# Attention in another order within its step, and one chain of Newton turns for two sets of row scalars

## The chip, the core and the metric

The kernel runs on one core of a Trainium2 chip. The time is device time in microseconds from start to end of one launch. The core has a matrix engine (TensorE, PE in the profile), a vector engine (VectorE, DVE), a scalar engine (ScalarE, ACT), GpSimd (POOL), and SyncE (SP), which here only issues transfers. Each engine works through its own instructions in the order in which they were written, and waits at an instruction until the semaphores that it names have reached a value.

## What is computed

Eight sequences of 512 tokens with 128 channels go through three residual stages: a mixture of experts, linear attention, and the same mixture of experts again.

```
x = x + 0.5 * ffn(layernorm(x))
x = x + attention(layernorm(x))
x = x + 0.5 * ffn(layernorm(x))

attention: q, k, v = x @ W.T + b, 16 heads of 8;  q = elu(q) + 1;  k = elu(k) + 1
           kv = sum_t k v ;  den = q . sum_t k ;  out = (q kv / max(den, 1e-6)) @ Wo.T + bo
ffn:       logits = x @ wg; the 2 best of 8 experts per token, each with room for 1024 tokens,
           h = relu(x @ w1 + b1); y = h @ w2 + b2; out = sum of the two, weighted
```

The second layernorm and routing work on the sum that attention leaves, so each sequence must be through attention before its tokens can be ranked and sent to their experts.

## The kernel before, in words

The program has four blocks: the first routing, the first experts, attention (with the second routing woven in), and the second experts. The change is in the attention block, at 171 to 308 us of the profiled execution.

**The step.** Attention goes over the NG = 8 sequences ("groups"), each as GT = 4 tiles of 128 tokens, in steps s = 0 to 7 and a tail. One step handles several groups in different phases. For the newest group s: VectorE adds the two expert results that GpSimd gathered (L910, `add_rows`), takes statistics (L1511), and works out the row scalars of the layernorm by three turns of a Newton iteration on 128x4 tiles (`scale_steps`, L1520 to L1547: each instruction waits for the one before it). ScalarE applies them (`norm`, L1431), TensorE turns the rows (`turn`, L1321), ScalarE copies them out (`anT_out`, L1439), TensorE makes q (L1328) and k, v (`kv`, L1337), ScalarE computes the exponentials (L1447 to L1461), and VectorE completes q and k (`q_sum` L1562, `k_sum` L1556). For group s-1: the key sum (`keysum`, L1349), the masking (`kv_mask`, L1569) and the answers (`query`, L1357). For group s-2: the division on VectorE (L1574 to L1585), the turning back (`turn_out`, L1365), the output projection (`project`, L1373 and L1377), the residual addition (L1591) and the statistics for the second routing (L1597). For s-3 and s-4: `route.turn` (L490), its copy (L449), and the routing's logits (`row_logits`, L502).

**The second routing** works in parts of two groups. Part 0 has its row scalars (`row_scalar_steps`, L273 to L315) in step 4 and its ranking (`top2_steps`, L586 to L620) in step 5; part 1 in steps 6 and 7; parts 2 and 3 in the tail. After a ranking, TensorE counts (`counts`, L742 to L749), and VectorE places and marks the rows (`place_steps`, `mark_steps`, to L822).

**GpSimd's queue.** It gathers 8 tiles for each group (L1269), one after another; after the last of them it sends the rows of part 0, 16 transfers (L839), and then those of parts 1 and 2 as they are marked. The second experts' block reads its first rows when these 48 are in.

**Order.** It is written out by hand: in `tensor`, `scalar` and `vector` of `Attention`, in a loop over s. On VectorE `advance(scale, n)` issues n more steps of the Newton chain at that place, `finish` all that are left. `fill` is a TensorE matmul on a constant, whose result is not used (L1312). Transposes of attention (L1321) and of the second routing (L490) share one bank of the accumulator memory (bank 0).

## Time and profile before

| | us |
|---|---|
| median of 3 runs | 473.25 |
| lowest and highest | 467.95, 474.01 |
| the profiled execution's own time | 469.24 |
| its span, first to last instruction | 467.5 |
| PE busy | 360.9 (77%) |
| DVE busy | 351.7 (75%) |
| POOL busy | 278.6 (60%) |
| ACT busy | 236.8 (51%) |

No engine is busy throughout. The chain that ended last is 54% PE, 11% DVE, 7% DMA and 6% POOL over the whole span; the shares are an average over stages with different limits, and the steps of attention have to be read by themselves. "Granted clock" is the share of full speed at which TensorE ran: 1.00 is 2.4 GHz, 0.50 is 1.2 GHz, and the trace has no other level.

### The profile page before, as it was taken

How to read it: one execution, taken by the hardware profiler on the slowest of the kernel's cores; microseconds unless marked ns; L12 is line 12 of the kernel's file. 1: busy time of each engine (PE TensorE's matmuls, PEld its weight loads, DVE VectorE, ACT ScalarE, POOL GpSimd, SP SyncE). 2: the span in 40 equal slices, each digit the busy share in tenths (PEclk: the TensorE clock that was granted, in tenths of full speed). 3: DMA queues.
4: the chain of work that ended last, by engine and by line, in shares of the span. 5: the costliest groups of instructions: out<-in, count | busy, mean ns of one | idle time of the engine just before them, and what ended most of it. 6: DMA issues, size and time to landing. Idle time of an engine off the chain costs nothing.

```text
span 467.5 us, 6299 instructions
## 1 busy us (share of the span) xinstructions
PE 360.9 (77%) x1830; PEld 287.1 (61%) x1830; DVE 351.7 (75%) x1083; ACT 236.8 (51%) x431; POOL 278.6 (60%) x303
## 2 busy tenths in 40 slices
PE   7932879999999975889877978505799999999300
PEld 6912548888888733667665758405588888888200
DVE  6889178998888864688878885840489889889483
ACT  3688147667776604455354471420466776666100
POOL 9000577666664457777754636677767777776720
PEclk9999989999999989799889795756899999999855
DMA  8940314666666341121110101111622232311599
GB/s 229 356 159 1 96 46 133 208 201 194 222 225 219 117 131 51 52 57 51 53 45 25 53 25 52 52 57 58 202 69 77 82 93 90 92 46 41 163 326 296
DMA packets 47265, 55.50 MB, mean 119 GB/s; under 512 B 6694, under 2 KB 32832, under 8 KB 47232
## 3 DMA queue, kind: packets, MB, share of 16 engines
q1 hardware_dynamic: 34352, 35.40, 22.9%
q0 software_dynamic: 8512, 17.60, 12.9%
q10 hardware_dynamic: 4368, 2.10, 1.5%
q8 instruction: 15, 0.25, 0.2%
q14 instruction: 18, 0.15, 0.1%
HBM read 25.98 MB, written 29.10 MB: 118 GB/s over the span
## 4 chain that ended last, share of the span: by engine, by line
PE 54%; DVE 11%; DMA 7%; POOL 6%; ACT 6%; issue 4%; POOLq 0%; ACTq 0%; DVEq 0%; SPq 0%
PE psum L1056 6%; PE psum L1052 6%; PE psum L1069 6%; PE psum L1067 6%; PE psum L1068 6%; PE psum L1053 6%; PE psum L1078 3%; PE psum L1039 3%; POOL xg L1025 3%; PE psum L1357 2%; PE psum L1312 2%; DMA xs_dram<-xns,place 2%; PE psum L1337 2%; DMA xns<-yt_dram 2%; ACT an L1431 2%
## 5 line engine op out<-in xcount | busy, mean ns | idle before, releaser
L1121 ACT ACTIVATE hf<-psum,bcol 128x512 f32<-128x512 f32 x128 | 88.5, 691 | 64.8 <-PE psum L1056 61.6
L1025 POOL DMA_INDIRECT xg<-xn_dram,gidx x64 | 68.0, 1062 | 67.1 <-POOLq L1702 37.5
L1158 DVE TENSOR_TENSOR hl<-hf,hh 128x512 fp32r<-128x512 f32 x128 | 87.2, 691 | 5.1 <-ACT hh L1123 2.2
L1011 POOL DMA_INDIRECT yt_dram<-yg,target x64 | 74.2, 1159 | 27.7 <-issue 16.6
L839 POOL DMA_INDIRECT xs_dram<-xns,place x64 | 63.5, 992 | 40.0 <-DMA xs_dram<-xns,place 15.7
L1269 POOL DMA_INDIRECT yg<-y_dram,slot x64 | 61.2, 957 | 30.2 <-issue 19.3
L1052 PE MATMUL psum<-xh,wres 128*128 128x512 f32 x128 | 54.1, 422 | 3.4 <-ACT xh L1106 3.4
L1067 PE MATMUL psum<-hh,wres 128*128 128x512 f32 x128 | 53.0, 414 | 0.0
L1056 PE MATMUL psum<-xl,wres 128*128 128x512 f32 x128 | 51.4, 402 | 0.1
L1053 PE MATMUL psum<-xh,wres 128*128 128x512 f32 x128 | 50.9, 398 | 0.0
L1069 PE MATMUL psum<-hh,wres 128*128 128x512 f32 x128 | 50.5, 395 | 0.0
L1068 PE MATMUL psum<-hl,wres 128*128 128x512 f32 x128 | 50.2, 393 | 0.0
L1151 DVE CAST hh<-hf 128x512 fp32r<-128x512 f32 x96 | 44.3, 462 | 6.3 <-ACT hf L1121 5.8
L1147 DVE TENSOR_TENSOR xl<-psum,xh 128x512 fp32r<-128x512 f32 x32 | 21.9, 683 | 31.0 <-ACT xh L1106 31.0
L1106 ACT CAST xh<-psum 128x512 fp32r<-128x512 f32 x32 | 18.8, 587 | 30.7 <-PE psum L1039 28.8
L1312 PE MATMUL psum<-ones_bf 128*128 128x512 bf16 x94 | 27.9, 428 | 2.2 <-PEq L1796 2.2
L1052 PEld LDWEIGHTS psum<-xh,wres 128*128 128x128 f32 x128 | 24.5, 192 | 8.3 <-ACT xh L1106 4.4
L1056 PEld LDWEIGHTS psum<-xl,wres 128*128 128x128 f32 x128 | 24.5, 192 | 7.2 <-DVE xl L1147 1.8
L1069 PEld LDWEIGHTS psum<-hh,wres 128*128 128x128 f32 x128 | 24.2, 189 | 5.5
L1053 PEld LDWEIGHTS psum<-xh,wres 128*128 128x128 f32 x128 | 24.7, 193 | 4.2
L1068 PEld LDWEIGHTS psum<-hl,wres 128*128 128x128 f32 x128 | 24.3, 190 | 4.2
L1067 PEld LDWEIGHTS psum<-hh,wres 128*128 128x128 f32 x128 | 24.3, 190 | 3.7
(247 smaller groups left out, 726.3 us busy)
## 6 DMA issues: line engine op xcount, KB each, us to landing
yt_dram<-zeros SPq DMA_DIRECT2D x24, 256.0 KB, 3.5
xns<-yt_dram SPq DMA_DIRECT2D x24, 256.0 KB, 5.0
xs_dram<-zeros SPq DMA_DIRECT2D x16, 288.0 KB, 2.7
xg<-xs_dram SPq DMA_DIRECT2D x16, 288.0 KB, 2.8
wexp_raw<-in_L_ffn_w SPq DMA_DIRECT2D x16, 256.0 KB, 6.2
y_dram<-y_rows_out SPq DMA_DIRECT2D x16, 256.0 KB, 2.4
x_sb<-in_L_attn_x SPq DMA_DIRECT2D x8, 256.0 KB, 4.1
xn_dram<-xns SPq DMA_DIRECT2D x8, 256.0 KB, 5.9
```

The source lines that it names most:

```text
L839: gp.indirect_dma_start(out=xs_dram, out_offset=bass.IndirectOffsetOnAxis(ap=self.place[:, k, t:t + 1], axis=0), in_=self.xns[:, t // GT, ...
L1011: gp.indirect_dma_start(out=yt_dram, out_offset=bass.IndirectOffsetOnAxis(ap=target[:, j:j + 1], axis=0), in_=self.y_sb[:, s % YG, t], in_ ...
L1025: gp.indirect_dma_start(out=self.xg[:, s % 4, t], out_offset=None, in_=xn_dram, in_offset=bass.IndirectOffsetOnAxis(ap=gidx[:, j:j + 1], a ...
L1052: nc.tensor.matmul(bank[1 + c][:], w[:, 0, at], self.xh[:, s % 2], start=True, stop=False)
L1053: nc.tensor.matmul(bank[1 + c][:], w[:, 2, at], self.xh[:, s % 2], start=False, stop=False)
L1056: nc.tensor.matmul(bank[1 + c][:], w[:, 0, at], self.xl[:, s % 2], start=False, stop=True).then_inc(h_ready[c], 1)
L1067: nc.tensor.matmul(sums[:], w[:, 1, at], self.hh[:, s % 2, c], start=(c == 0), stop=False)
L1068: nc.tensor.matmul(sums[:], w[:, 1, at], self.hl[:, s % 2, c], start=False, stop=False)
L1069: last = nc.tensor.matmul(sums[:], w[:, 3, at], self.hh[:, s % 2, c], start=False, stop=(c == HC - 1))
L1121: one = nc.scalar.activation(self.hf[:, c], bank[1 + c][:], ACT.Relu, bias=bcol[:, at:at + 1])
L1158: dve.tensor_tensor(self.hl[:, s % 2, c], self.hf[:, c], self.hh[:, s % 2, c].bitcast(F32), ALU.subtract).then_inc(hl_ready[c], 1)
L1269: gp.indirect_dma_start(out=self.yg[:, n % YB, k, t], out_offset=None, in_=y_dram, in_offset=bass.IndirectOffsetOnAxis(ap=slot[:, k, GT * ...
```

## The change

On TensorE a step now has, after its four fills: `turn_out`, `keysum`, `row_logits`, `turn`, `project`, `route.turn`, two fills, `q`, `kv`, `query`, `counts`. The four fills between `query` and `q` are gone (28 in seven steps). The routing's turned rows use bank 6 instead of bank 0 up to group 4, and the waits follow that. On ScalarE `raw_out` and `anT_out` come ahead of the routing's copy. On VectorE the whole Newton chain of group s is issued ahead of `q_sum` and `k_sum`. In steps 4 and 6 the routing's row scalars are no longer a chain of 24 instructions: they are 8 `bn_aggr` and then columns 4 to 11 of the attention's own chain, which is 12 wide there.

```diff
--- before.py
+++ after.py
@@ -358,6 +358,10 @@
             act.wait_ge(WT_ps, 2)
             nc.scalar.copy(WT[:, 0:3].rearrange("p w c -> p (w c)"), bank[7][:, 0:3 * C]).then_inc(WT_sb, 1)
 
+        def rows_bank(g):
+
+            return bank[6] if g < NG - 3 else bank[0]
+
         def logit_bank(g):
 
             return bank[2] if g < NG // 2 else bank[6]
@@ -446,7 +450,7 @@
                 act.wait_ge(turned, NG * f + g + 1)
                 if g >= 2:
                     act.wait_ge(logits_done, NG * f + g - 1)
-                nc.scalar.copy(self.xT[:, g % 2], (turn_bank(g) if f == 0 else bank[0])[:]).then_inc(xnT_ready, 1)
+                nc.scalar.copy(self.xT[:, g % 2], (turn_bank(g) if f == 0 else rows_bank(g))[:]).then_inc(xnT_ready, 1)
 
             def raw_out(self, act, g):
 
@@ -482,10 +486,11 @@
                         pe.wait_ge(xnT_ready, g - 1)
                 else:
                     pe.wait_ge(x_summed, g + 1)
-                    pe.wait_ge(anT_ready, min(g + 3, NG))
+                    if g >= NG - 3:
+                        pe.wait_ge(anT_ready, NG)
                     if g >= 1:
                         pe.wait_ge(xnT_ready, NG + g)
-                to = turn_bank(g) if f == 0 else bank[0]
+                to = turn_bank(g) if f == 0 else rows_bank(g)
                 for t in range(GT):
                     last = nc.tensor.transpose(to[:, t * P:(t + 1) * P], x_sb[:, GT * g + t], ident[:])
                 last.then_inc(turned, 1)
@@ -1301,8 +1306,8 @@
                 self.att = new("att", [P, 2, GT, C])
                 self.attT = new("attT", [P, 2, SEQ])
                 self.sta = new("sta", [P, 2, GT, 6])
-                self.agg = new("agg", [P, 2, GT, 2])
-                self.nwa = new("nwa", [P, 2, 3, GT])
+                self.agg = new("agg", [P, 2, GT + PT, 2])
+                self.nwa = new("nwa", [P, 2, 3, GT + PT])
                 self.rsa = new("rsa", [P, 2, 2, GT])
 
             def tensor(self, pe):
@@ -1315,8 +1320,6 @@
                     pe.wait_ge(an_ready, n + 1)
                     if n >= 1:
                         pe.wait_ge(anT_ready, n)
-                    if n >= 3:
-                        pe.wait_ge(xnT_ready, NG + n - 2)
                     for t in range(GT):
                         last = nc.tensor.transpose(bank[0][:, t * P:(t + 1) * P], self.an[:, n % 2, t], ident[:])
                     last.then_inc(an_turned, 1)
@@ -1361,6 +1364,8 @@
                     pe.wait_ge(att_ready, n + 1)
                     if n >= 1:
                         pe.wait_ge(attT_ready, n)
+                    if n >= 2:
+                        pe.wait_ge(xnT_ready, NG + min(n - 1, NG - 3))
                     for t in range(GT):
                         last = nc.tensor.transpose(bank[6][:, t * P:(t + 1) * P], self.att[:, n % 2, t], ident[:])
                     last.then_inc(att_turned, 1)
@@ -1381,30 +1386,26 @@
                 for s in range(NG):
                     if s >= 1:
                         fill(0, 4)
+                    if s >= 2:
+                        turn_out(s - 2)
+                    if s >= 1:
+                        keysum(s - 1)
+                    if s >= 4:
+                        self.route.row_logits(pe, s - 4)
+                    turn(s)
+                    if s >= 2:
+                        project(s - 2)
                     if s >= 3:
                         self.route.turn(pe, s - 3)
-                    if s >= 2:
-                        turn_out(s - 2)
-                    if s >= 4:
-                        self.route.row_logits(pe, s - 4)
-                    if s >= 1:
-                        keysum(s - 1)
-                    if s >= 2:
-                        project(s - 2)
-                    turn(s)
                     if s >= 1:
                         pe.wait_ge(qT_ready, s)
                         fill(1, 2)
+                    q(s)
+                    kv(s)
+                    if s >= 1:
                         query(s - 1)
-                        fill(1, 4)
                     if s in (5, 7):
                         self.route.counts(pe, (s - 5) // 2)
-                    if s < NG - 1:
-                        q(s)
-                        kv(s)
-                    else:
-                        kv(s)
-                        q(s)
 
                 self.route.turn(pe, NG - 3)
                 turn_out(NG - 2)
@@ -1471,19 +1472,19 @@
                         q_act(s - 1)
                         k_act(s - 1)
                     if s == NG:
+                        q_act(NG - 1)
                         k_act(NG - 1)
-                        q_act(NG - 1)
-                    if s >= 4:
+                    if s == NG:
                         self.route.raw_out(act, s - 4)
                     if s >= 2:
                         attT_out(s - 2)
                     if s < NG:
                         norm(s)
+                        if s >= 4:
+                            self.route.raw_out(act, s - 4)
+                        anT_out(s)
                     if s >= 3:
                         self.route.turned_out(act, s - 3)
-                    if s < NG:
-                        anT_out(s)
-
                     if s in (5, 7):
                         self.route.scalar_norm(act, s - 5)
                         self.route.scalar_norm(act, s - 4)
@@ -1514,14 +1515,20 @@
                 def scale_steps(n):
 
                     u = n % 2
-                    v, y, a = (self.nwa[:, u, q] for q in range(3))
+                    part = {4: 0, 6: 1}.get(n)
+                    m = GT if part is None else GT + PT
+                    v, y, a = (self.nwa[:, u, q, 0:m] for q in range(3))
+                    if part is not None:
+                        ch.wait()
+                        for t in range(PT):
+                            ch.add(dve.bn_aggr(self.agg[:, u, GT + t], stats[:, PT * part + t]))
                     dve.wait_ge(an_stats, n + 1)
                     for t in range(GT):
                         ch.add(dve.bn_aggr(self.agg[:, u, t], self.sta[:, u, t]))
                     done = ch.n
                     yield
                     ch.wait(done)
-                    ch.add(dve.tensor_scalar(v, self.agg[:, u, :, 1], EPS, None, ALU.add))
+                    ch.add(dve.tensor_scalar(v, self.agg[:, u, 0:m, 1], EPS, None, ALU.add))
                     done = ch.n
                     yield
 
@@ -1539,12 +1546,21 @@
                         done = ch.n
                         yield
                         ch.wait(done)
-                        to = self.rsa[:, u, 0] if square == 4.0 else y
-                        ch.add(dve.scalar_tensor_tensor(to, a, -3.0, y, ALU.add, ALU.mult))
-                        done = ch.n
+                        if square == 4.0:
+                            ch.add(dve.scalar_tensor_tensor(self.rsa[:, u, 0], a[:, 0:GT], -3.0, y[:, 0:GT], ALU.add, ALU.mult))
+                            done = ch.n
+                            if part is not None:
+                                ts = slice(PT * part, PT * part + PT)
+                                ch.add(dve.scalar_tensor_tensor(rstd[:, ts], a[:, GT:m], -3.0, y[:, GT:m], ALU.add, ALU.mult))
+                        else:
+                            ch.add(dve.scalar_tensor_tensor(y, a, -3.0, y, ALU.add, ALU.mult))
+                            done = ch.n
                         yield
                     ch.wait(done)
-                    dve.scalar_tensor_tensor(self.rsa[:, u, 1], self.agg[:, u, :, 0], -1.0, self.rsa[:, u, 0], ALU.mult, ALU.mult).then_inc(an_scale, 1)
+                    dve.scalar_tensor_tensor(self.rsa[:, u, 1], self.agg[:, u, 0:GT, 0], -1.0, self.rsa[:, u, 0], ALU.mult, ALU.mult).then_inc(an_scale, 1)
+                    if part is not None:
+                        ch.wait()
+                        dve.scalar_tensor_tensor(nmr[:, ts], self.agg[:, u, GT:m, 0], -1.0, rstd[:, ts], ALU.mult, ALU.mult).then_inc(rstd_done, 1)
                     yield
 
                 def k_sum(n):
@@ -1597,8 +1613,7 @@
                         ch.add(dve.bn_stats(stats[:, t], x_sb[:, t]))
 
                 route = self.route
-                others_at = {4: row_scalar_steps(ch, dve, 0, PT), 5: route.top2_steps(dve, ch, 0),
-                             6: row_scalar_steps(ch, dve, PT, 2 * PT), 7: route.top2_steps(dve, ch, 1)}
+                others_at = {5: route.top2_steps(dve, ch, 0), 7: route.top2_steps(dve, ch, 1)}
                 for s in range(NG):
                     others = others_at.get(s, iter(()))
                     add_rows(dve, s, 1)
@@ -1612,14 +1627,14 @@
                         advance(scale, 1)
                         divide(s - 2)
                         advance(scale, 1)
-                    if s == NG - 1:
-                        finish(scale)
+                    for _ in scale:
+                        if s in (4, 6):
+                            advance(others, 1)
                     if s >= 1:
                         q_sum(s - 1)
-                        advance(scale, 3)
                         k_sum(s - 1)
-                    for _ in scale:
-                        advance(others, 2)
+                    if s in (4, 6):
+                        advance(others, 5)
                     if s >= 1:
                         kv_mask(s - 1)
                     finish(others)
@@ -1639,8 +1654,8 @@
                 den_inverse(NG - 2)
                 divide(NG - 2)
                 advance(scalars, 6)
+                q_sum(NG - 1)
                 k_sum(NG - 1)
-                q_sum(NG - 1)
                 kv_mask(NG - 1)
                 advance(scalars, 6)
                 den_max(NG - 1)
```

Two places show how it moves instructions. The first is PE, step 6, from the routing's turn to the fills that end the step. Before (`ident,an` is attention's turn, `ident,x_sb` the routing's, `ident,att` the turning back, `vv,kk` the key sum, `kv,qT` the query):

```order
L490 MATMUL psum<-ident,x_sb 128x128 x4
L1365 MATMUL psum<-ident,att 128x128 x4
L502 MATMUL psum<-wgc,xT 128x8 x4
L1349 MATMUL psum<-vv,kk 128x129 x4
L1373 MATMUL psum<-bpair,ones 128x512
L1377 MATMUL psum<-WT,attT 128x128 x4
L1321 MATMUL psum<-ident,an 128x128 x4
L1312 MATMUL psum<-ones_bf 128x512 x2
L1357 MATMUL psum<-kv,qT 128x144 x4
L1312 MATMUL psum<-ones_bf 128x512 x4
L1328 MATMUL psum<-anT,WT 128x512
L1337 MATMUL psum<-WT,anT 128x256 x4
```

And now, the same work of step 6:

```order
L1370 MATMUL psum<-ident,att 128x128 x4
L1352 MATMUL psum<-vv,kk 128x129 x4
L507 MATMUL psum<-wgc,xT 128x8 x4
L1324 MATMUL psum<-ident,an 128x128 x4
L1378 MATMUL psum<-bpair,ones 128x512
L1382 MATMUL psum<-WT,attT 128x128 x4
L495 MATMUL psum<-ident,x_sb 128x128 x4
L1317 MATMUL psum<-ones_bf 128x512 x2
L1331 MATMUL psum<-anT,WT 128x512
L1340 MATMUL psum<-WT,anT 128x256 x4
L1360 MATMUL psum<-kv,qT 128x144 x4
```

`project` (L1378, L1382) has moved behind attention's turn, the logits behind the key sum, and the query behind k and v.

The second place is DVE, step 4, from the first Newton instruction to `k_sum`. Before, `k_sum` (`kk`) has four of them ahead of it:

```order
L1534 SCALAR_TENSOR_TENSOR nwa<-nwa 128x4 [waits dve_step]
L1562 SCALAR_TENSOR_TENSOR qT<-psum,qe 128x512 [waits num_ready,q_parts]
L1538 TENSOR_TENSOR nwa<-nwa 128x4 [waits dve_step]
L1543 SCALAR_TENSOR_TENSOR nwa<-nwa 128x4 [waits dve_step]
L1534 SCALAR_TENSOR_TENSOR nwa<-nwa 128x4 [waits dve_step]
L1556 SCALAR_TENSOR_TENSOR kk<-psum,ke 128x512 [waits keysum_ready,v_copied,k_parts]
```

Now all of them are:

```order
L1545 TENSOR_TENSOR nwa<-nwa 128x12 [waits dve_step]
L1550 SCALAR_TENSOR_TENSOR rsa<-nwa 128x4 [waits dve_step]
L1554 SCALAR_TENSOR_TENSOR rstd<-nwa 128x8
L1560 SCALAR_TENSOR_TENSOR rsa<-agg,rsa 128x4 [waits dve_step]
L1563 SCALAR_TENSOR_TENSOR nmr<-agg,rstd 128x8 [waits dve_step]
L1578 SCALAR_TENSOR_TENSOR qT<-psum,qe 128x512 [waits num_ready,q_parts]
L1572 SCALAR_TENSOR_TENSOR kk<-psum,ke 128x512 [waits keysum_ready,v_copied,k_parts]
```

Nothing of the chain is left for the time after `k_sum`.

## Rows read from the trace of the kernel before

**Rows 1.** Timeline, POOL: start, duration, engine, line, operation, [idle before, releaser].

```profile
241.33 0.95 POOL L1269 DMA_INDIRECT yg<-y_dram,slot  x1 [0.30 <-issue]
...
279.93 0.97 POOL L839 DMA_INDIRECT xs_dram<-xns,place  x1 [7.20 <-DVE xns L822]
```

**Rows 2.** Chain of waits, one piece: start us, us, what.

```profile
326.45 2.67 DMA xg<-xs_dram
```

**Rows 3.** Timeline, DVE, step 3.

```profile
205.42 0.87 DVE L1511 BATCH_NORM_STATS2 sta<-x_sb 128x6 f32<-128x128 f32 x4
206.33 0.38 DVE L1520 BATCH_NORM_AGGREGATE agg<-sta 128x2 f32<-128x6 f32 x4
...
210.15 0.69 DVE L1556 SCALAR_TENSOR_TENSOR kk<-psum,ke 128x512 f32<-128x512 f32 x1 [0.89 <-ACT vv L1461]
...
213.61 0.69 DVE L1591 TENSOR_TENSOR x_sb<-psum,x_sb 128x512 f32<-128x512 f32 x1
...
216.28 0.87 DVE L1511 BATCH_NORM_STATS2 sta<-x_sb 128x6 f32<-128x128 f32 x4
```

**Rows 4.** Timeline, DVE: start of step 2, and step 7.

```profile
193.64 0.87 DVE L1511 BATCH_NORM_STATS2 sta<-x_sb 128x6 f32<-128x128 f32 x4
...
262.20 0.87 DVE L1511 BATCH_NORM_STATS2 sta<-x_sb 128x6 f32<-128x128 f32 x4
...
265.01 0.16 DVE L1538 TENSOR_TENSOR nwa<-nwa 128x4 f32<-128x4 f32 x1
...
266.66 0.69 DVE L1562 SCALAR_TENSOR_TENSOR qT<-psum,qe 128x512 f32<-128x512 f32 x1
...
270.46 0.26 DVE L575 COPY pick<-before 128x16 bf16<-128x16 bf16 x1
...
274.55 0.68 DVE L1591 TENSOR_TENSOR x_sb<-psum,x_sb 128x512 f32<-128x512 f32 x1
...
276.86 0.53 DVE L773 SCALAR_TENSOR_TENSOR prod<-psum,pick 128x64 f32<-128x64 f32 x3
...
278.91 0.27 DVE L822 SCALAR_TENSOR_TENSOR xns<-share,gap 128x64 f32<-128x64 f32 x1
```

**Rows 5.** Timeline, PE, where the granted clock is high.

```profile
200.04 1.16 PE L1349 MATMUL psum<-vv,kk 128*128 128x129 f32 x8 [1.32 <-DVE kk L1556]
...
214.19 0.63 PE L1321 MATMUL psum<-ident,an 128*128 128x128 f32 x4 [0.61 <-ACT xT L449]
...
216.93 1.02 PE L1328 MATMUL psum<-anT,WT 128*128 128x512 f32 x2
...
221.25 0.96 PE L502 MATMUL psum<-wgc,xT 128*128 128x8 f32 x8
222.28 1.16 PE L1349 MATMUL psum<-vv,kk 128*128 128x129 f32 x8
...
223.80 1.16 PE L1377 MATMUL psum<-WT,attT 128*128 128x128 f32 x8
```

**Rows 6.** Timeline, ACT, step 3.

```profile
214.86 0.60 ACT L1439 ACTIVATE anT<-psum 128x512 f32<-128x512 f32 x1 [0.81 <-PE psum L1321]
```

**Rows 7.** Timeline, PE, around the stretches at the low clock.

```profile
227.15 0.63 PE L1321 MATMUL psum<-ident,an 128*128 128x128 f32 x4 [2.19 <-ACT xT L449]
...
242.27 1.08 PE L1321 MATMUL psum<-ident,an 128*128 128x128 f32 x4 [2.68 <-ACT xT L449]
...
256.89 2.08 PE L1377 MATMUL psum<-WT,attT 128*128 128x128 f32 x8
...
282.69 2.05 PE L1349 MATMUL psum<-vv,kk 128*128 128x129 f32 x8 [0.60 <-DVE kk L1556]
...
287.27 1.71 PE L502 MATMUL psum<-wgc,xT 128*128 128x8 f32 x8
```

**Rows 8.** Windows: us, busy us of PE, PEld, DVE, ACT, POOL, granted clock.

```profile
195.00:227.00 32.00, 27.01 (x157) 20.21 (x155) 26.29 (x123) 17.61 (x35) 24.04 (x26) 1.00 0.20 53
255.80:262.40 6.60, 6.00 (x24) 4.64 (x23) 6.29 (x34) 2.72 (x6) 4.82 (x5) 0.51 0.15 48
```

## Prediction, written before the changed kernel ran

> **What bounds the kernel now.** I read the end first and went backwards. The second experts start with the read of their first rows at 326.45 [rows 2], which waits until GpSimd has sent the rows of parts 0, 1 and 2. GpSimd's sends of parts 1 and 2 run without a pause from 279.93, and ahead of them it sat idle for 7.20 us, released by VectorE's last mark of step 7 [rows 1]. That mark starts at 278.91 and takes 0.27 [rows 4]: 279.18 is the time that counts. What comes later in attention (part 2's marks) has some microseconds to spare against this queue, and everything behind hangs on it. So a change of attention is worth what it moves the marks of step 7, one for one.
>
> At the front end the steps start with GpSimd's gather. The statistics of step 2 start at 193.64 [rows 4], just after the rows of group 2 have landed, and no order of the engines can make that earlier. The last gather is issued at 241.33 [rows 1], while step 7 starts only at 262.20 [rows 4]: from step 3 on the gather is ahead, and the engines' own order is the limit. I count from 193.64 to the marks of step 7, 85.5 us before.
>
> Within a step I read VectorE's and TensorE's timelines side by side. In step 3 (205.42 to 216.28, 10.86 us) VectorE waits 0.89 for the copy of v ahead of `kk` [rows 3]. This is the wait that the new order attacks: q and k are now made straight after `turn`, without four fills and a query in between.
>
> **The change, part by part: the step at the high clock.** The new loop runs through VectorE again and again, so I follow it from one `sta` to the next.
>
> 1. From `sta` to `q_sum`. The new order issues the whole Newton chain first. Step 7 of the kernel before already has this very order: 262.20 to 266.66, 4.46 us [rows 4].
> 2. `q_sum` holds the engine 0.61 (0.69 less the 0.08 by which a row overlaps the next), then `k_sum` takes 0.69 and TensorE's `keysum` starts 0.06 later: 0.75. That `k_sum` doesn't wait for ScalarE any more is right, but it now starts 4.46 + 0.61 = 5.07 after `sta`, against 210.15 - 205.42 = 4.73 before [rows 3]. The 0.89 of waiting used to hold part of the chain; now the chain stands in front in full.
> 3. From `keysum` to the residual addition. `project` now stands behind `turn`: 1.52 from `keysum` to the start of `project`'s own matmuls, 1.16 for those [rows 5], 0.5 for `turn` (its 0.63 less what overlaps), 0.04 to release: 3.2. VectorE has only the masks and four `add_rows` for this time, and waits for the rest. Before, the chain lay in part of it, and `project` came earlier.
> 4. From the residual addition to the next `sta`: 213.61 to 216.28, 2.67 [rows 3].
>
> The sum is 4.46 + 0.61 + 0.75 + 3.2 + 2.67 = 11.7, against 10.86 before: the loop loses 0.8, since two waits (masks, residual) have taken the place of one. Steps 2 and 3 are such steps. From step 4 on, `row_logits` stands between `keysum` and `turn`: 221.25 to 222.28, 1.03 more [rows 5].
>
> In steps 4 and 6 the joined chain adds 8 `bn_aggr` at 0.075 (four take 0.38 [rows 3]) and two wide instructions, 0.7 together; being 12 wide and not 4 costs nothing that I price. The 24 instructions of the old chain go. Those steps come to 11.7 + 1.0 + 0.7 = 13.4.
>
> Step 5 has 5.8 to `keysum` (items 1 and 2). From there VectorE needs 2.3 until the raw logits are copied, 4.09 for ranking and gaps (270.46 to 274.55), 1.05 for four `add_rows`, 2.3 until it wants the counts (274.55 to 276.86): 9.8. TensorE's counts now stand behind `query`: 1.0 + 2.7 + 0.5 for logits, key sum, `project` and `turn`, and about the 4.3 from 216.93 to 221.25 [rows 5], where nearly the same work stands: 8.6, just hidden. Then 2.3 to the last mark, 1.2 for `add_rows`: 19.1. Step 7 is the same without the `add_rows`: 5.8 + 8.8 + 2.3 = 16.9 to its last mark.
>
> Sum: 193.64 + 2 x 11.7 + 2 x 13.4 + 19.1 + 16.9 = 279.8, against 279.18. At the high clock the change would be worth +0.7 us: what the joined chain saves in steps 4 and 6 is spent on the loop.
>
> **The clock.** From 195 to 227 TensorE was granted the full clock; from 255.80 to 262.40 half of it [rows 8]. TensorE's idle times in the first stretch are short (1.32 ahead of a key sum, [rows 5]). Idle times of 2.19 and 2.68 [rows 7] stand directly at the start of stretches at 1.2 GHz: the `turn` behind the second takes 1.08 in place of 0.63. Now the new step: `turn_out` can start when the division ends, some 2.8 after `sta`; `keysum` starts 5.8 after it. Less the 0.44 of `turn_out`, that is an idle time of 2.6 us in every step, with a further one ahead of `turn_out`, and 28 fills are gone. The old order had such waits in steps 4 and later only. I expect a low stretch in every step from 2 on, and just behind the idle time, where `keysum`, `row_logits`, `turn` and `project` now stand in the loop of VectorE. At the low clock a key sum takes 2.05 and not 1.16, the logits 1.71 and not 0.96, `project` 2.08 and not 1.16, `turn` 1.08 and not 0.63 [rows 5, 7]. Extra: 0.89 + 0.92 + 0.45 = 2.3 in steps 2 and 3; with the logits 3.0 in steps 4 and 6. In steps 5 and 7 VectorE waits for the counts: between 3.0 and 3.0 + 4.3 = 7.3, if all that stands ahead of the counts is at the low clock; less up to 1.2 of slack. I take 5 each. Sum: 4.6 + 6.0 + 10 = 20.6.
>
> Edits at nothing: bank 6 for the routing's turn, and the changed waits (each is on work long done; were `turn_out` held by the copy of the routing's rows, it would be inside the idle time ahead of `keysum`). ScalarE's new order matters in steps 5 and 7 alone, where 8 norms stand ahead of q's exponentials; ScalarE is then done some 3 us later, still ahead of the later `q_sum`. If that cover is gone it costs 1 to 2 us.
>
> **Total.** 0.7 + 20.6 = +21.3 on the marks, on GpSimd's sends and on the end. The profiled execution took 469.24; 490.5. The median of the three runs is 4.0 above it (473.25), so I forecast 492, between 490.5 and 494.5.
>
> One rule of the Trainium skill can be weighed here. The rows show that each chained instruction issues 0.195 after the one before (265.01 to 266.66, 8 spaces and one of 0.08 [rows 4]), while four independent `bn_aggr` are 0.075 apart [rows 3]. The Trainium skill, page "VectorE: DVE Perf Modes", section "The DRAIN you can't avoid", says that a semaphore after each instruction costs nothing more than one at the end. By it the 8 spaces put ahead of `k_sum` would cost 8 x 0.12 = 1.0 less in each of six steps, and the estimate would be 486; the trace disagrees and I go by the rows.
>
> **Rivals.**
> - *The clock stays high.* Four fills still follow `query`, and the idle time is split by `turn_out`. Then only +0.7 is left: 470 by the profile's own time, up to 474. Against it: idle times no longer than the new one stand ahead of the low stretches in the trace. If it falls in half of the steps, +11: 480 to 485.
> - *Faster.* The wait for ScalarE is the true bound, and the new order takes it out. Place: between `turn` and `q`, 216.93 - 214.19 = 2.74 before; now `turn` (0.63) and the copy of 0.60 [rows 5, 6] are left with some 0.1: 1.4 saved a step, 8.6 in six, 460.6. GpSimd's idle 7.20 [rows 1] and an earlier part 0 would let it through. It decides as soon as VectorE reaches `k_sum` before ScalarE has v ready; by item 2 it reaches it 0.3 later than now, so the saved time should lie as slack on ScalarE.
> - *The change does nothing:* the loop's +0.7 and a clock that falls as often as before. That is the first rival's time, 470 to 474.
>
> **Chances.** The forecast (484 to 504) 0.72; clock low in half of the steps 0.10; clock high or nothing changed 0.11; faster 0.07. Bounds of the forecast: steps 5 and 7 at 3.0 each give -4, at 7 each +4, the median's 4.0, and 1 to 2 from ScalarE; all of it on one side gives 504. Downwards 478 takes in the half case. 2 in 10 or less lie outside 478 to 504. A measurement of this kernel can tell about 2%, 9.5 us: slower than 482.7 with 0.80 (the forecast and most of the half case), within with 0.13, faster than 463.8 with 0.07.
>
> **What would show it.** Right: `kk` without a wait for ScalarE; VectorE idle ahead of the masks (for the key sum) and of the residual addition (for `project`); granted clock under 0.8 from 200 to 300 us; step lengths of 13 to 17 us and over 20 in step 5; the last mark of step 7 near 300; and the sends and the second experts as before, only shifted. Wrong: a granted clock near 1 from 200 to 240, steps of 11.7, or `kk` earlier than 4.7 after `sta`. Most would be wrong if the length of an idle time alone doesn't make the clock fall.

## The result

| | before | changed |
|---|---|---|
| median, and its runs | 470.75 us (5) | 496.19 us (5) |
| lowest and highest | 467.95, 474.01 | 489.33, 499.86 |
| profiled execution | 469.24 | 490.1 |
| its span | 467.5 | 488.4 |

The ratio is 1.045, with a 95% interval of 1.040 to 1.051: slower. The comparison leaves disturbed runs out, which is why the ratio is below 496.19 / 470.75 = 1.054.

**The profile after.** First the page: span, busy times, and the granted clock over 40 equal slices.

```profile
span 488.4 us, 6222 instructions
...
PE 369.2 (76%) x1802; PEld 295.5 (61%) x1802; DVE 351.6 (72%) x1063; ACT 237.2 (49%) x431; POOL 272.8 (56%) x303
...
PEclk9999979999999987979756667755899999999955
```

TensorE's share of the span is what it was (76% against 77%), with 28 fills fewer: 369.2 us busy and not 360.9. Fewer instructions took more time, since more of them ran at 1.2 GHz. In the clock's row the slices from the 20th to the 27th (some 232 to 330 us) read 7, 5, 6, 6, 6, 7, 7, 5.

Where the time went is found as it was for the kernel before, from the queue that holds the end. POOL's timeline, the first send of part 0 and the first of parts 1 and 2 ([rows 1] has the latter):

```profile
261.33 1.01 POOL L844 DMA_INDIRECT xs_dram<-xns,place  x1 [17.91 <-DVE xns L827]
...
302.07 0.96 POOL L844 DMA_INDIRECT xs_dram<-xns,place  x1 [17.80 <-DVE xns L827]
```

The second burst starts at 302.07 and not at 279.93. The statistics of step 2 start at 193.74 against 193.64 [rows 4], so the whole loss, 108.33 - 86.29 = 22.0 us, is between these two marks. Behind them nothing is lost: 488.4 - 302.07 = 186.3 against 467.5 - 279.93 = 187.6. The same stretch as a window (its start and end, its length in us, then busy us and instructions of PE, PEld, DVE, ACT and POOL, the granted clock, DMA share, GB/s):

```profile
193.74:302.07 108.33, 82.02 (x381) 63.15 (x379) 69.64 (x317) 47.03 (x98) 52.32 (x55) 0.76 0.13 36
```

The clock is 0.76; the kernel before has 0.92 in its own such stretch, 193.64 to 279.93. Now DVE in step 3, which answers to [rows 3], and four rows, one being the start of step 4 and three of steps 5 to 7:

```profile
207.08 0.87 DVE L1512 BATCH_NORM_STATS2 sta<-x_sb 128x6 f32<-128x128 f32 x4
...
212.35 0.68 DVE L1572 SCALAR_TENSOR_TENSOR kk<-psum,ke 128x512 f32<-128x512 f32 x1
214.86 0.29 DVE L1585 TENSOR_TENSOR kv<-psum,block_mask 128x128 f32<-128x128 f32 x1 [1.83 <-PE psum L1352]
...
218.44 0.69 DVE L1607 TENSOR_TENSOR x_sb<-psum,x_sb 128x512 f32<-128x512 f32 x1 [2.16 <-PE psum L1382]
...
221.11 0.87 DVE L1512 BATCH_NORM_STATS2 sta<-x_sb 128x6 f32<-128x128 f32 x4
...
258.07 0.53 DVE L778 SCALAR_TENSOR_TENSOR prod<-psum,pick 128x64 f32<-128x64 f32 x3 [2.09 <-PE psum L754]
...
261.44 0.87 DVE L1512 BATCH_NORM_STATS2 sta<-x_sb 128x6 f32<-128x128 f32 x4
...
277.76 0.87 DVE L1512 BATCH_NORM_STATS2 sta<-x_sb 128x6 f32<-128x128 f32 x4
```

`kk` has no wait any more, as intended. But it starts 212.35 - 207.08 = 5.27 after `sta` (4.73 before), and two waits have come, 1.83 for the key sum and 2.16 for `project`. The row at 258.07 waits 2.09 for the counts of step 5. And TensorE in the same step, which answers to [rows 5, 7]:

```profile
210.00 0.66 PE L1370 MATMUL psum<-ident,att 128*128 128x128 f32 x4 [0.77 <-DVE att L1601]
213.08 1.74 PE L1352 MATMUL psum<-vv,kk 128*128 128x129 f32 x8 [2.43 <-DVE kk L1572]
214.62 1.06 PE L1324 MATMUL psum<-ident,an 128*128 128x128 f32 x4
...
216.32 2.08 PE L1382 MATMUL psum<-WT,attT 128*128 128x128 f32 x8
```

The idle time of 2.43 ahead of the key sum is there in every step (2.37, 2.43, 2.52, 2.38, 2.07 and 2.38 in steps 2 to 7), with 0.77 ahead of `turn_out` besides (5.70 in step 6). Behind it, from step 3 on, stands the low clock: `turn` 1.06 and `project` 2.08, against 0.63 and 1.16 [rows 5]. In this row the clock falls within the key sum (1.74, between 1.16 and 2.09). VectorE waits for exactly these.

Step 2 is the exception. The same idle time stands there, and no low stretch follows; the granted clock of the whole step is 1.00:

```profile
201.26 1.16 PE L1352 MATMUL psum<-vv,kk 128*128 128x129 f32 x8 [2.37 <-DVE kk L1572]
...
203.21 1.16 PE L1382 MATMUL psum<-WT,attT 128*128 128x128 f32 x8
```

It takes 13.3 us all the same, 1.5 more than before. VectorE has a third new wait there, at the start of the division, for the query (L1360), which now stands behind q, k and v. The kernel before has no such wait in these steps. Steps 2 and 5:

```profile
196.64 0.22 DVE L1590 TENSOR_SCALAR den<-psum 128x64 f32<-128x64 f32 x1 [1.61 <-PE psum L1360]
...
240.31 0.23 DVE L1590 TENSOR_SCALAR den<-psum 128x64 f32<-128x64 f32 x1 [2.11 <-PE psum L1360]
```

In steps 4 and 7 it is 1.09 and 2.17.

The steps from one `sta` to the next, 2 to 6, in us, and the stretch from `sta` of step 2 to the second burst:

| kernel | step 2 | 3 | 4 | 5 | 6 | stretch | clock in it |
|---|---|---|---|---|---|---|---|
| before | 11.8 | 10.9 | 13.5 | 20.5 | 12.0 | 86.3 | 0.92 |
| changed | 13.3 | 14.0 | 15.8 | 24.5 | 16.3 | 108.3 | 0.76 |

### The profile page after: what moved, and what is told of

Same layout as the page of the kernel before. It is cut to its first block and busy times, and to the rows that moved or that the text cites. A ratio compares the mean times of both kernels' runs of the same rounds, so it can differ in the third digit from the quotient of the medians.

```text
span 488.4 us, 6222 instructions
## 1 busy us (share of the span) xinstructions
PE 369.2 (76%) x1802; PEld 295.5 (61%) x1802; DVE 351.6 (72%) x1063; ACT 237.2 (49%) x431; POOL 272.8 (56%) x303
## 5 line engine op out<-in xcount | busy, mean ns | idle before, releaser
L1030 POOL DMA_INDIRECT xg<-xn_dram,gidx x64 | 66.2, 1035 | 69.1 <-POOLq L1717 37.7
L1016 POOL DMA_INDIRECT yt_dram<-yg,target x64 | 71.0, 1110 | 28.4 <-issue 16.6
L1274 POOL DMA_INDIRECT yg<-y_dram,slot x64 | 61.2, 956 | 31.2 <-issue 18.9
L1057 PEld LDWEIGHTS psum<-xh,wres 128*128 128x128 f32 x128 | 24.5, 192 | 9.1 <-ACT xh L1111 5.1
L507 PEld LDWEIGHTS psum<-wgc,xT 128*128 128x128 f32 x128 | 27.3, 315 | 2.9 <-ACT xT L453 2.7
L1352 PE MATMUL psum<-vv,kk 128*128 128x129 f32 x64 | 14.5, 397 | 19.2 <-DVE kk L1572 19.2
L507 PE MATMUL psum<-wgc,xT 128*128 128x8 f32 x128 | 26.3, 336 | 1.9 <-ACT xT L453 1.9
L1074 PEld LDWEIGHTS psum<-hh,wres 128*128 128x128 f32 x128 | 24.2, 189 | 5.5
```

Source lines behind the costliest of these rows:

```text
L1016: gp.indirect_dma_start(out=yt_dram, out_offset=bass.IndirectOffsetOnAxis(ap=target[:, j:j + 1], axis=0), in_=self.y_sb[:, s % YG, t], in_ ...
L1030: gp.indirect_dma_start(out=self.xg[:, s % 4, t], out_offset=None, in_=xn_dram, in_offset=bass.IndirectOffsetOnAxis(ap=gidx[:, j:j + 1], a ...
L1057: nc.tensor.matmul(bank[1 + c][:], w[:, 0, at], self.xh[:, s % 2], start=True, stop=False)
L1074: last = nc.tensor.matmul(sums[:], w[:, 3, at], self.hh[:, s % 2, c], start=False, stop=(c == HC - 1))
L1274: gp.indirect_dma_start(out=self.yg[:, n % YB, k, t], out_offset=None, in_=y_dram, in_offset=bass.IndirectOffsetOnAxis(ap=slot[:, k, GT * ...
```

## The experiments

Theory, from the prediction: the order by itself costs about nothing, and some 21 us come from the clock, which falls behind the new idle time of TensorE. Rivals: the loop through VectorE is longer by itself; the missing fills lower the clock, wherever they stood; VectorE's order alone, or TensorE's alone, does it. Each time stands with its ratio to the kernel before in runs on the same chip, and 95% interval.

**1. Fills in the idle time of the changed kernel** (`e1_warm`).

```diff
                     if s >= 2:
                         turn_out(s - 2)
+                        fill(0, 10)
                     if s >= 1:
                         keysum(s - 1)
```

> The changed kernel with ten more fills in every step from 2 on, issued right behind turn_out, where TensorE waits 2.4 to 2.6 us for k; nothing else differs. Theory (the low clock carries the loss, 20 of 21 us): the granted clock stays near 1 from 200 to 300 us, the last mark of step 7 falls from 301 to 280 to 285, and the time to 470 to 476. Rival (the new order itself carries the loss, through its longer loop on VectorE): the time stays at 490 to 500.

Measured: 473.06 us (10 runs), 1.009 (1.004 to 1.015). Ten more matmuls in each of six steps made the changed kernel some 17 us faster by the ratios (1.009 against 1.045), and 19 by the profiled executions (470.83 against 490.1). Its steps 2 to 6 take 13.1, 11.8, 13.2, 19.3 and 13.9. DVE, step 3; POOL, the second burst; and the window up to it:

```profile
205.50 0.87 DVE L1513 BATCH_NORM_STATS2 sta<-x_sb 128x6 f32<-128x128 f32 x4
...
217.33 0.87 DVE L1513 BATCH_NORM_STATS2 sta<-x_sb 128x6 f32<-128x128 f32 x4
```

```profile
281.89 0.97 POOL L844 DMA_INDIRECT xs_dram<-xns,place  x1 [9.94 <-DVE xns L827]
```

```profile
192.42:281.89 89.47, 74.99 (x440) 53.32 (x438) 69.88 (x317) 46.91 (x98) 52.31 (x55) 0.96 0.16 44
```

The instructions that do the work, and their order, are those of the changed kernel; what differs is the fills, and with them the clock, 0.96 against 0.76. (The expectation of a clock near 1 up to 300 us holds only to the second burst; from 200 to 300 it is 0.88, for behind the burst key sums of 2.09 are left.) So the clock is the cause of most of the loss, and the loop at the high clock is the small term: 89.5 us in place of 86.3.

**2. Half as many fills** (`e18_warm5`): the same edit with `fill(0, 5)`.

> The changed kernel with 5 fills behind turn_out in place of 10: the idle time ahead of the key sum is then 1.3 to 1.5 us and not 2.4 to 2.6. Theory (short idle times don't lower the clock, long ones do): closer to the kernel with ten fills (473) than to the changed one (496): 474 to 484, with a spread of several us between runs. Rival (any gap at that place lowers it): 488 or more.

Measured: 475.11 (5), 1.011 (1.007 to 1.015). The window, and TensorE's row in step 3:

```profile
192.37:284.01 91.64, 71.73 (x409) 52.36 (x407) 69.80 (x317) 46.67 (x98) 52.36 (x55) 0.93 0.15 42
```

```profile
211.21 1.16 PE L1352 MATMUL psum<-vv,kk 128*128 128x129 f32 x8 [1.40 <-DVE kk L1573]
```

With the idle time cut from 2.4 to 1.3 to 1.5 a step, most of the clock is back (0.93). That is 2 us above ten fills, with intervals that overlap: five are about enough.

**3. TensorE's order alone** (`e2_chain_split`): the changed kernel, with VectorE's chain around `q_sum` and `k_sum` again.

```diff
-                    for _ in scale:
-                        if s in (4, 6):
-                            advance(others, 1)
                     if s >= 1:
                         q_sum(s - 1)
+                        advance(scale, 3)
                         k_sum(s - 1)
-                    if s in (4, 6):
-                        advance(others, 5)
+                    finish(scale)
```

> The changed kernel with VectorE's Newton chain split around k_sum again: four chained instructions ahead of k_sum, the rest right behind it, ahead of the masks. TensorE, ScalarE and the joined chain stay as changed. Theory: keysum starts 1.6 us earlier after the statistics, TensorE's idle time ahead of it shrinks from 2.4 to about 1 us where ScalarE lets it, so fewer low stretches: 483 to 492. Rival (TensorE's new order is the fault, not VectorE's): 494 to 498, no change from the changed kernel.

Measured: 484.97 (4), 1.031 (1.020 to 1.043), the runs from 480.2 to 494.1. The profiled one is the slowest, so its rows overstate this kernel's low clock: over the whole execution its granted clock is 0.85, and that of the other three 0.87 to 0.89. Its window, and TensorE in step 3:

```profile
196.68:302.95 106.27, 84.06 (x381) 63.68 (x379) 68.79 (x317) 46.95 (x98) 52.05 (x56) 0.75 0.13 36
```

```profile
217.36 1.43 PE L1352 MATMUL psum<-vv,kk 128*128 128x129 f32 x8 [1.14 <-DVE kk L1572]
220.09 1.11 PE L1324 MATMUL psum<-ident,an 128*128 128x128 f32 x4 [1.30 <-ACT an L1432]
```

`kk` comes 0.9 to 1.9 us earlier after `sta` than in the changed kernel, but for step 3 (5.42 for 5.27), and the idle time is split: 1.14 ahead of the key sum, and 1.30 ahead of `turn`, which now waits for the norm. In this execution the clock is as low as in the changed kernel. What the ratio says without it: a loss of 3.1% is there with VectorE's chain split, so the whole chain ahead of `k_sum` is not needed for the greater part of the loss. The other edits of the change suffice for that, TensorE's and ScalarE's order, the joined chain and the missing fills together. Whether VectorE's position of the chain is worth the rest is not shown, since the intervals overlap (1.020 to 1.043 against 1.040 to 1.051).

**4. The same with fills** (`e6_split_warm`): experiment 3 with `fill(0, 8)` behind `turn_out`.

> The changed kernel with both repairs: the Newton chain split around k_sum again, and eight fills behind turn_out. What is left of the change is TensorE's and ScalarE's order and the joined chain, at a high clock. Theory: the loop is then about as long as before; last mark of step 7 at 279 to 283, time 469 to 474. Rival (VectorE's order is the whole loss at the high clock, TensorE's a gain of some 2 us a step, as meant): 462 or less.

Measured: 473.51 (10), 1.009 (1.005 to 1.013), against 473.06 for the unsplit chain with fills.

```profile
193.94:282.85 88.91, 72.39 (x428) 52.94 (x426) 68.79 (x317) 46.55 (x98) 52.41 (x55) 0.96 0.16 44
```

At the high clock these runs show no difference between the two places of VectorE's chain. (There are eight fills a step here, and ten in experiment 1.)

**5. VectorE's order alone** (`e4_vector_order_only`): the kernel before, its TensorE untouched.

```diff
-                    if s == NG - 1:
-                        finish(scale)
+                    for _ in scale:
+                        advance(others, 2)
                     if s >= 1:
                         q_sum(s - 1)
-                        advance(scale, 3)
                         k_sum(s - 1)
-                    for _ in scale:
-                        advance(others, 2)
```

> The kernel before with VectorE's new order alone: the whole Newton chain ahead of q_sum and k_sum, in steps 4 and 6 with the old 24-instruction chain woven into it; TensorE and ScalarE as before, the chains not joined. Theory (the chain ahead of k_sum makes TensorE's long idle time, which lowers the clock in every step): 483 to 491, with a granted clock under 0.85 from 200 to 300 us. Rival (only both orders together do it): 471 to 476, for the 1 us a step that k_sum comes later.

Measured: 485.54 (4), 1.035 (1.026 to 1.045). TensorE's key sums in steps 2 to 5:

```profile
200.04 1.16 PE L1349 MATMUL psum<-vv,kk 128*128 128x129 f32 x8 [1.32 <-DVE kk L1556]
...
211.31 1.16 PE L1349 MATMUL psum<-vv,kk 128*128 128x129 f32 x8 [1.55 <-DVE kk L1556]
...
224.85 2.09 PE L1349 MATMUL psum<-vv,kk 128*128 128x129 f32 x8 [3.04 <-DVE kk L1556]
...
243.95 2.09 PE L1349 MATMUL psum<-vv,kk 128*128 128x129 f32 x8 [5.71 <-DVE kk L1556]
```

In steps 2 and 3 the idle time is 1.3 and 1.6, the key sums take 1.16, and the steps (12.0 and 11.3) cost 0.2 and 0.4 more than before. These two steps have VectorE's new order with nothing woven in, as the change has it, and there it costs next to nothing. From step 4 on the idle time is 3.0 to 5.7, and the key sum 2.09. There this kernel overstates VectorE's part: the routing's old chain and the ranking, two instructions for each of the attention's, also went ahead of `k_sum`, which the change does not do. What stands is that idle times of 3.0 to 5.7, longer than the change's 2.1 to 2.5, have the low clock behind them with all fills in place.

**6, 7. Are the missing fills the cause?** (`e9_no_fills_behind_query`, `e10_no_fills`) The kernel before without the four fills behind the query, and without any of the ten fills of a step. The last line below is the edit of the first, all three are that of the second.

```diff
-                        fill(0, 4)
...
-                        fill(1, 2)
                         query(s - 1)
-                        fill(1, 4)
```

> The kernel before without the four fills between query and q (28 in all), everything else as before. Theory (it is the long idle time ahead of the key sum that lowers the clock, and the old order hasn't got it): q and kv start 0.86 earlier a step, one or two more low stretches: 465 to 473. Rival (the changed kernel's clock falls because 28 fills are missing): 480 or more, with a granted clock under 0.85 from 200 to 300 us.

> The kernel before without any fill in the steps (ten a step; the 24 at the start stay). Theory: TensorE's idle times grow by what the fills took, in several pieces of 1 to 2 us, so more steps fall to the low clock, while 2 us a step leave TensorE's path: 466 to 480. Rival (fills as such keep the clock, wherever they stand): 485 or more.

Measured: 468.39 (10), 0.997 (0.993 to 1.001); and 461.90 (4), 0.983 (0.979 to 0.988). The first is as the theory has it: in the old order the 28 fills that the change drops are not needed for the time, though the profiled execution has a clock of 0.87 from `sta` of step 2 to the second burst, where before has 0.92. No run puts these 28 back into the new order, so a part of theirs in its low clock is not ruled out. The second misses its expectation on the fast side. DVE's step 3, TensorE, and the window:

```profile
204.17 0.87 DVE L1507 BATCH_NORM_STATS2 sta<-x_sb 128x6 f32<-128x128 f32 x4
...
214.09 0.87 DVE L1507 BATCH_NORM_STATS2 sta<-x_sb 128x6 f32<-128x128 f32 x4
```

```profile
208.70 1.16 PE L1349 MATMUL psum<-vv,kk 128*128 128x129 f32 x8 [1.11 <-DVE kk L1552]
...
213.49 1.02 PE L1328 MATMUL psum<-anT,WT 128*128 128x512 f32 x2
...
223.77 0.63 PE L1321 MATMUL psum<-ident,an 128*128 128x128 f32 x4 [2.26 <-ACT xT L449]
...
236.02 1.08 PE L1321 MATMUL psum<-ident,an 128*128 128x128 f32 x4 [2.41 <-ACT xT L449]
...
245.67 0.76 PE L1365 MATMUL psum<-ident,att 128*128 128x128 f32 x4 [3.18 <-DVE att L1581]
```

```profile
192.82:271.97 79.15, 62.01 (x338) 51.16 (x336) 70.91 (x337) 46.02 (x98) 52.27 (x56) 0.88 0.18 49
```

Step 3 takes 9.9 and not 10.9. TensorE's q starts 213.49 - 204.17 = 9.3 after `sta`, against 216.93 - 205.42 = 11.5 before [rows 5, 3]. The fills stood between the copy of the turned rows and q, which is in the loop, and they held q back. The clock does fall, 0.88 against 0.92, with `turn` at 1.08 behind idle times of 2.4, but this costs less than the fills did. The kernel before paid more for its clock than the clock was worth.

**8, 9. The joined chain alone** (`e3_join_only`, and `e15_join_no_fills`, which has no fills either): the kernel before with the change's `scale_steps`. The lines shown take the old chain out of steps 4 and 6; those of `scale_steps` are as in the change.

```diff
-                others_at = {4: row_scalar_steps(ch, dve, 0, PT), 5: route.top2_steps(dve, ch, 0),
-                             6: row_scalar_steps(ch, dve, PT, 2 * PT), 7: route.top2_steps(dve, ch, 1)}
+                others_at = {5: route.top2_steps(dve, ch, 0), 7: route.top2_steps(dve, ch, 1)}
```

> The kernel before with the joined chain alone: steps 4 and 6 have 8 bn_aggr and 12-wide Newton instructions in place of the 24 instructions; all orders as before. Theory: steps 4 and 6 get 1.5 to 2 us shorter at the high clock, part of it lost again to waits: 466 to 471. Rival (by the rule that instructions count, not their waits, 20 fewer instructions of 0.16 in each of two steps): 464, 6 us faster.

> The kernel before with the joined chain and without any fill in the steps. The kernel without fills alone took 461.9, the joined chain alone 470.2 against 470.4. Theory: at the high clock the joined chain shortens steps 4 and 6 by 1.5 to 3 us together, and with the fills gone VectorE is the path there, so it shows now: 458 to 462. Rival (a longer idle time of TensorE in those steps lowers the clock more often and takes it back): 462 to 468.

Measured: 470.23 (10), 1.002 (0.998 to 1.005); and 460.97 (4), 0.981 (0.976 to 0.985). DVE's step 4 of the first:

```profile
219.17 0.87 DVE L1511 BATCH_NORM_STATS2 sta<-x_sb 128x6 f32<-128x128 f32 x4
...
224.50 0.69 DVE L1571 SCALAR_TENSOR_TENSOR kk<-psum,ke 128x512 f32<-128x512 f32 x1 [1.06 <-ACT vv L1461]
...
230.63 0.87 DVE L1511 BATCH_NORM_STATS2 sta<-x_sb 128x6 f32<-128x128 f32 x4
```

The joined chain makes step 4 11.46 long and not 13.5, so the 24 instructions were on the path there. The end does not move: `sta` of step 7 starts at 264.42 and not at 262.20, after steps 2, 3 and 6 that are longer (13.7, 11.6 and 13.1). The clock from 193 to 219 is 0.87, where before has 0.98, and 0.61 from 252 to 264, against 0.72. Steps 2 and 3 stand ahead of the first joined chain, so their longer time is not its work, and this profiled execution is the slowest of the ten (472.18). That ten runs as a whole show no gain (1.002) is sure; what took the 2.0 of step 4 back in them is not shown. Without the fills, DVE's step 4 and the window:

```profile
213.91 0.87 DVE L1507 BATCH_NORM_STATS2 sta<-x_sb 128x6 f32<-128x128 f32 x4
...
224.23 0.87 DVE L1507 BATCH_NORM_STATS2 sta<-x_sb 128x6 f32<-128x128 f32 x4
```

```profile
192.57:271.22 78.65, 61.70 (x338) 50.61 (x336) 67.59 (x317) 45.31 (x98) 52.25 (x55) 0.88 0.17 49
```

Step 4 is 10.3 (12.3 without the join). This is the fastest kernel of the study, ahead of both. Its lead over `e10_no_fills` is 0.9 us, with overlapping intervals; that the join is worth anything at the end is not shown.

**10 to 12. Can the clock be had more cheaply?** Three placements of fills in TensorE's idle times, with the old order. `e13_join_fills_moved` has the join, and its four fills behind the query moved to the wait ahead of `turn`:

```diff
                     if s >= 2:
                         project(s - 2)
+                        fill(6, 4)
                     turn(s)
...
                         query(s - 1)
-                        fill(1, 4)
```

> The kernel before with the joined chain, and with the four fills behind query moved to the place behind project, where TensorE waits for attention's rows (into bank 6, which is free there). Orders of all other work as before. Theory: 0.86 a step leaves the path from turn to q, the joined chain is worth 1.7 in steps 4 and 6, and the fills stand in the idle time: last mark of step 7 at 272 to 277 in place of 279, time 463 to 470. Rival (GpSimd's and VectorE's waits take it back): 470.

`e16_join_fills_in_wait` is `e15_join_no_fills` with `fill(6, 8)` in that place, and `e7_before_warm` the kernel before, all its fills kept, with eight there from step 4 on and 16 more in step 1.

> As the one before (joined chain, no fills ahead of or behind other work), but with 8 fills behind project in each step from 2 on, where TensorE waits for attention's rows. Theory (fills help the clock where there is a wait and cost their own time where there is none): 460 to 464, the wait of 1 to 2.4 us being longer than the 1.7 of the fills in steps 4 to 6 only. Rival (a steadier clock is worth more than the path they take): under 458.

> The kernel before with 8 more fills behind project in steps 4 to 7 (into bank 6, ahead of the wait for attention's rows), and 16 more ahead of the first key sum in step 1; nothing removed or moved. Theory: the low stretches of steps 1, 4, 5 and 6 go, last mark of step 7 at 273 to 276, time 464 to 469. Rival (those low stretches lie beside other waits): 470.

Measured: 462.44 (4), 0.984 (0.980 to 0.989); 467.37 (6), 0.990 (0.986 to 0.995); 466.50 (4), 0.989 (0.983 to 0.995). The window of the first, and a key sum of the second:

```profile
192.59:273.31 80.72, 70.78 (x400) 53.26 (x399) 68.23 (x317) 45.87 (x98) 52.25 (x56) 0.93 0.18 48
```

```profile
212.42 1.16 PE L1349 MATMUL psum<-vv,kk 128*128 128x129 f32 x8 [1.73 <-DVE kk L1568]
```

The first came out just under its 463 to 470. It keeps a clock of 0.93 and is level with no fills at all at 0.88 (0.980 to 0.989 against 0.976 to 0.985): what the clock gives back and what the fills take come to about the same here. Against the joined chain with the fills in their old place (470.23), moving four a step is worth nearly 8 us.

The second missed the theory's 460 to 464: eight fills in the wait cost 6 us against none, at a clock of 0.90, with an idle time of 1.73 still ahead of the key sum. Its rows say where. In step 3 the wait ahead of `turn` is 0.61 without fills, and the eight hold TensorE for 1.73. First `e15_join_no_fills`, then `e16_join_fills_in_wait`:

```profile
211.82 0.63 PE L1321 MATMUL psum<-ident,an 128*128 128x128 f32 x4 [0.61 <-ACT xT L449]
```

```profile
214.93 1.89 PE L1312 MATMUL psum<-ones_bf 128*128 128x512 bf16 x8
216.66 0.60 PE L1321 MATMUL psum<-ident,an 128*128 128x128 f32 x4
```

From the start of the key sum `turn` starts 216.66 - 212.42 = 4.24 later, and 3.29 without fills; in step 4 it is 4.24 against 3.33. So the expectation took the wait as 1 to 2.4 where it is 0.6, and the rest of the fills stood on the path.

The third is a gain of 1% from fills alone, with the same work.

## Why the prediction was right

**The bound.** That the marks of step 7 set the end, one for one, held nearly: 22.1 us later at the second burst, 20.9 in the profiled time. Some 1.2 were made up behind the burst; by what was not looked into. The start of step 2, which I took as fixed by the gather, lies between 192.37 and 196.69 in the profiled executions, so two kernels are better compared by stretches that start at a `sta` than by the marks themselves.

**The step at the high clock.** `e1_warm` is the measurement of it. Forecast 11.7, 13.4, 19.1, 13.4 for steps 3 to 6 and 16.9 to the last mark; measured 11.8, 13.2, 19.3, 13.9, and 17.4 less the 0.7 from the mark to the burst, 16.7. Only step 2 is off, 13.1 for 11.7. It began earlier, at 192.42, with step 3 at 205.50 in its old place (205.42), but the changed kernel's step 2 began at 193.74 and took 13.3, at a granted clock of 1.00. What the prediction left out there is VectorE's wait for the query, 1.29 in `e1_warm` and 1.61 in the changed kernel: the division needs the query, and the query's new place behind q, k and v has no price in the sum. The term was mis-sized besides: +0.7 was forecast, and from `sta` of step 3 to the burst it is 76.4 against 74.5, +1.9; by the medians +2.6. The parts: `kk` at 5.27 after `sta` for 5.07, and the key sum at 6.0 for 5.8.

**The clock.** Forecast: a low stretch in every step from 2 on, directly behind the idle time of 2.6. Measured: idle times of 2.1 to 2.5, low stretches in steps 3 to 7 and none in step 2, granted clock 0.76, and the lengths of the low matmuls as taken (2.09, 1.71, 1.09, 2.08). Extra by steps, changed kernel less `e1_warm`: step 2 +0.3 (2.3 forecast), step 3 +2.2 (2.3), step 4 +2.6 (3.0), step 5 +5.2 and step 7 +6.2 (5 each), step 6 +2.4 (3.0). VectorE's wait for the counts, 2.09, is in step 5 as forecast, and absent in `e1_warm`.

Not all of it comes by the forecast path, the matmuls behind the key sum. From `sta` to `kk` the changed kernel takes 1.0, 1.6 and 1.7 longer than `e1_warm` in steps 4, 5 and 7, where VectorE waits 1.1 to 2.2 for the query. That is 4.3 of the 18.9, through a wait that the prediction did not have, and behind `kk` its terms were too large: in step 4, 1.6 for 3.0, since the key sum still took 1.16 there and the low clock began behind it.

The measured clock share of the loss is 108.3 - 89.5 = 18.9 us, where the sum had 20.6; the order's share is 3.2, where the sum had 0.7; and 1.2 were made up behind the burst. So 490.5 met the profiled 490.1 by errors that cancel. That the clock carries most of the loss was foreseen; the closeness of the number is luck.

**The median.** I put it 4.0 above the profiled execution, which is what three runs of the kernel before had; with two more runs that one's median is 1.5 above its own. The changed kernel's is 6.1 above, inside the range. One profiled execution does not show how far the runs spread, here from 489.33 to 499.86.

**The Trainium skill's rule**, as I applied it, would have given 486. In the changed kernel the chained instructions still issue some 0.2 apart (210.04, 210.24, 210.44, 210.63), and `kk` in step 3 came 0.2 later than forecast, not 1.0 earlier. The page "VectorE: DVE Perf Modes", section "The DRAIN you can't avoid", of the Trainium skill compares one chain of copies with and without semaphores, and I had read it too widely. No run here takes the semaphores out of the chain, and the `bn_aggr` 0.075 apart are another operation, so how much of the 0.2 is the wait is not shown.

**The rivals.** In the new order the clock stayed high only where fills were put into the idle time, and then the time was 473 to 475, about that rival's 470 to 474. The faster one fell at its own point: VectorE reaches `k_sum` later than ScalarE has v, which was done at 209.16 (208.59 and 0.57) in step 3, 3.2 ahead of `kk`. The time that ScalarE's wait used to take is slack there.

What I did not see is that the fills of the kernel before cost time themselves. I took them as pure cover; `e10_no_fills` says that they were on the path.

**Still open.** What in TensorE's past decides the clock: in the changed kernel an idle time of 2.37 had no low stretch behind it (step 2), and in `e4_vector_order_only` one of 1.6 had none, while in `e2_chain_split` two of 1.1 and 1.3 had one. Also open are VectorE's share of the loss from step 4 on, where it was tried only with more woven in than the change has, and the share of the missing fills in the new order.

## What to carry to other kernels

Before moving an instruction that a loop waits for, read how long the matrix engine will stand idle ahead of it, and price what stands behind that idle time at the low clock: an order that is only 2 to 3 us longer cost 21. Where such an idle time can't be avoided, a few matmuls in it, where the engine waits anyway, give most of it back; the same matmuls ahead of work that the loop waits for can cost more than the clock they keep, so try the kernel without them too. And a step that gets shorter is not yet a gain: in `e3_join_only` step 4 is 2.0 us shorter and the whole is not faster.

## What was not expected of the hardware

Two idle times of 1.14 and 1.30 us in a step of 15 us went with a granted clock of 0.75 in the slowest execution of `e2_chain_split`, while a single one of 1.3 to 1.5 us a step left it at 0.93 in `e18_warm5`. Ten fills a step raised the clock from 0.88 to 0.92 and made the kernel 1.7% slower (`e10_no_fills` against before), while ten fills in another place raised it from 0.76 to 0.96 and made the kernel 19 us faster (`e1_warm`, profiled executions). So the mean granted clock of a stretch ranks neither kernels nor placements; the fastest kernel of the study, 460.97, has 0.88.
